# The gated transposition six products into the third part, and the lora products of the first two parts at eighteen products instead of twelve

## The reference

```python
# layer 0: one low-rank adapter (rank 16) per sequence
Bx  = einsum('bni,bri->bnr', x, B0[adapter_id])
x1  = x + einsum('bnr,bor->bno', Bx, A0[adapter_id])
# layer 1: a dense product and a gated mixture of 8 low-rank experts (rank 16)
base   = einsum('btd,od->bto', x1, W)
logits = einsum('btd,ed->bte', x1, Wr) + 5 * one_hot(lang_id)
gates  = softmax over the two largest logits, spread over the 8 experts
h      = einsum('btd,erd->bter', x1, A1)
out    = x1 + base + 2 * einsum('bter,bte,eor->bto', h, gates, B1)
```

## Time and profile before

| | |
|---|---|
| median of three runs | 525.92 us (523.71 to 525.93) |
| the profiled execution's own time | 527.19 us |
| its span, first to last instruction | 525.4 us |
| TensorE matmul busy | 510.3 us, 97% |
| VectorE busy | 382.2 us, 73% |
| ScalarE busy | 240.7 us, 46% |
| GpSimd busy | 172.2 us, 33% |
| mean granted TensorE clock | 0.997 of full speed |

### The profile page before, as it was taken

How to read it: one execution, slowest core, us unless ns; L and a number is a source line. 1 busy time by engine, 2 the same in 40 slices (tenths; PEclk the granted TensorE clock), 3 DMA queues, 4 the chain that set the end, 5 groups by cost and what they waited for, 6 DMA issues and landing times.

```text
span 525.4 us, 9426 instructions
## 1 busy us (share of the span) xinstructions
PE 510.3 (97%) x3350; PEld 464.4 (88%) x3350; DVE 382.2 (73%) x879; ACT 240.7 (46%) x543; POOL 172.2 (33%) x162
## 2 busy tenths in 40 slices
PE   6898999999999999999999999999999999999997
PEld 5787999878989899999989899998989999888997
DVE  3877786658669696977969697796969789694441
ACT  4645433445354544445454445455444545543221
POOL 6360325633414434132334414143442414330000
PEclk9999999999999999999999999999999999999999
DMA  8954255736667868567785857767675876632301
GB/s 331 311 132 110 90 133 170 205 112 217 227 186 204 243 179 253 177 210 238 249 246 150 252 182 232 233 210 248 180 234 177 249 207 211 201 120 82 121 40 41
DMA packets 52467, 99.76 MB, mean 190 GB/s; under 512 B 6716, under 2 KB 35260, under 8 KB 52420
## 3 DMA queue, kind: packets, MB, share of 16 engines
q1 hardware_dynamic: 45744, 78.14, 48.6%
q0 software_dynamic: 6656, 20.98, 12.3%
q10 hardware_dynamic: 20, 0.03, 0.0%
HBM read 69.24 MB, written 29.88 MB: 189 GB/s over the span
## 4 chain that ended last, share of the span: by engine, by line
PE 81%; DVE 10%; issue 4%; ACT 3%; another core or an unknown queue 1%; POOL 1%; DMA 0%; ACTq 0%; DVEq 0%
PE o_bank L601 64%; PE o_bank L614 8%; PE b_bank L493 2%; PE x_bank L521 2%; PE o_bank L590 2%; DVE a_raw L935 1%; PE b_bank L478 1%; ACT bx_pair L750 1%; DVE x_bank L900 1%; DVE b_raw L925 1%; PE o_bank L478 1%; PE x_bank L478 1%; DVE top_no L995 1%; ACT bx_swap L743 1%
## 5 line engine op out<-in xcount | busy, mean ns | idle before, releaser
L601 PE MATMUL o_bank<-w_hi,x_hi 128*128 128x512 f32 (+1 forms) x744 | 255.6, 344 | 0.0
L601 PE MATMUL o_bank<-w_lo,x_hi 128*128 128x512 f32 (+1 forms) x744 | 251.1, 337 | 0.0
L601 PE MATMUL o_bank<-w_hi,x_lo 128*128 128x512 f32 (+1 forms) x744 | 250.9, 337 | 0.0
L409 POOL TENSOR_TENSOR a_t<-a_raw,a_t 64x1024 fp32r<-64x1024 f32 x30 | 72.4, 2412 | 250.1 <-ACT a_t L723 177.5
L601 PEld LDWEIGHTS o_bank<-w_hi,x_hi 128*128 128x128 f32 x744 | 140.0, 188 | 13.4 <-issue 3.0
L601 PEld LDWEIGHTS o_bank<-w_lo,x_hi 128*128 128x128 f32 x744 | 139.9, 188 | 10.1
L601 PEld LDWEIGHTS o_bank<-w_hi,x_lo 128*128 128x128 f32 x744 | 139.7, 188 | 10.2
L380 POOL DMA_INDIRECT a_in<-in_L_cond_A_dram,a_run x64 | 60.9, 952 | 19.2 <-issue 18.7
L723 ACT CAST a_t<-a_raw 128x1024 fp32r<-128x1024 f32 x32 | 33.6, 1051 | 71.3 <-DVE a_raw L935 71.2
L935 DVE STREAM_TRANSPOSE a_raw<-a_in 128x1024 f32<-128x1024 f32 x32 | 65.3, 2045 | 0.0
L797 ACT COPY out_sb<-o_bank 128x376 f32<-128x376 f32 (+2 forms) x96 | 39.3, 443 | 54.4 <-PE o_bank L614 54.3
(11 more groups left out here) (110 smaller groups left out, 503.5 us busy)
## 6 DMA issues: line engine op xcount, KB each, us to landing
out_dram<-out_sb SPq DMA_DIRECT2D x31, 512.0 KB
x_in<-in_x_dram SPq DMA_DIRECT2D x120, 128.0 KB
w_in<-in_x_dram SPq DMA_DIRECT2D x25, 512.0 KB
x_dram<-w_in SPq DMA_DIRECT2D x25, 512.0 KB, 4.8
w_in<-x_dram SPq DMA_DIRECT2D x100, 128.0 KB
w_in<-in_L_cond_W_dram SPq DMA_DIRECT2D x6, 512.0 KB, 13.9
x_in<-in_x_dram SPq DMA_DIRECT2D x2, 512.0 KB
out_sb<-in_L_cond_W_dram SPq DMA_DIRECT2D x2, 512.0 KB, 14.6
```

What stands on the lines that cost most here:

```text
L409: nc.gpsimd.tensor_tensor(lower, a_raw[Q:P, m % 2, :], lower.bitcast(F32), ALU.subtract)\
L601: mm = pe.matmul(O[part][:, 0:hi - lo], xs[:, n % 2, c, :], w[:, c, lo:hi], start=(k == 0), stop=(k == K3 - 1), skip_group_check=True)
```

## The change

In every tile from 1 on, the first 6 products of part 2 are put ahead of `turn_gated`. The lora products of parts 0 and 1 stand 12 products behind the transposition, as they did, which is now at 18 of the 24 products of part 2, so that 6 of them are left behind instead of 12. Nothing is added or removed: TensorE has the same instructions in another order, and the orders of the other engines are as before. Tile 0, which is written out by itself, is not touched.

```diff
                 make_part(n, 1, 0, K3)
+                make_part(n, 2, 0, 6)
                 turn_gated(n)
-                make_part(n, 2, 0, 12)
+                make_part(n, 2, 6, 18)
                 pe.wait_ge(gt_ready, 2 * (n + 1))
                 add_lora(0)
                 add_lora(1)
-                make_part(n, 2, 12, K3)
+                make_part(n, 2, 18, K3)
                 add_lora(2)
```

## The result

The changed kernel takes 528.53 us (median of 15 runs, 526.50 to 531.18), the kernel before, beside it on the same chip, 525.69 (15 runs, 523.71 to 526.93): ratio 1.0059, 95% interval 1.0040 to 1.0078. It is slower by 2.8 us; forecast was 528.5. The profiled execution of after, 526.50 us with a span of 524.7, happens to be one of its two shortest, and is shorter than the profiled one of before. So the two traces must be compared stretch by stretch, not by their ends. That the forecast and the median agree to 0.03 us is luck in part: the interval of the ratio allows a change of 2.1 to 4.1 us.

A forecast was written before the change was run, and what follows sets the result against it. TensorE bounds the kernel (matmuls in 97% of the span). Early tiles −0.20, nine pairs +3.1, tile 28 −0.74 gave +2.1 us; without hold-ups +3.2; the middle, +2.6, gave 528.5 us, range 524.7 to 531.0.

The forecast's parts named there:

- The step, 0.89 us, and the delay of `gt_hi`: Six products put the transposition 0.89 us later; `gt_hi`, 0.31 behind it, moves 0.89 in odd tiles, 0.66 in even.
- A: Even tiles: TensorE's weight load for `make_x1` newly waits for GpSimd's late `a_t`; 0.15 us each, bounds 0 and 0.42.
- B: Even tiles: second half of the two-`make_bx` group newly waits for VectorE's `b_raw`; 0.19 us each, bounds 0 and 0.3.
- ScalarE's exponential behind the rounding of `a_t`: Even tiles: ScalarE's rounding, 0.89 us later, holds the exponential, which moves `gated` and L914 by 0.7.
- Later lora products cost nothing: Long regular stretch: next tile's `x_lo` and the copies out of PSUM come later but still in time, cost 0.
- The early tiles: Up to tile 9: tile 2 gains 0.47 us, tiles 4 and 5 nothing more, standing at −0.20 at tile 9.
- Tile 28: Two TensorE waits there are covered up to 0.89 us; `gt_lo` comes 0.15 later, so −0.74.
- The hold-ups look like chance: VectorE's in tiles 4 and 28, ScalarE's in 7: without them +3.2 us instead of +2.1; the middle, +2.6, taken.
- The signs: Trace: `gated` wait left in tile 5 alone, `gt_hi` waiting nearly everywhere, L493 group about 1.3, transposition distance +2.7 us.
- Rival 1: TensorE's waits for `gated` and `gt_lo` go and nothing replaces them: 3.9 us gained, 522.1 us; chance 0.07.
- rival 2: `a_t` and `b_raw` have room after all: only −0.3 to −1.2 us is left, about 525.2 us; chance 0.17.
- rival 3: Room is smaller, a pair costing 0.54, or hold-ups hit slackless paths: +4.0 to +5.3, about 530.5 us; chance 0.21.

The follow-up runs named there:

- fix6_odd: Changed kernel with VectorE's `gated_t_part` moved behind both halves L914 in odd tiles too, even tiles unaltered; 529.64 us, 1.0024 of the kernel before.
- odd6: Changed kernel with the move kept in odd tiles only, even tiles having transposition at 0 and lora at 12; 530.16 us, 1.0028 of the kernel before.
- even6: Changed kernel with transposition and lora products moved in even tiles only; 531.37 us, 1.0064 of the kernel before.
- turn0_lora18: Changed kernel with the transposition back ahead of part 2, only the lora products moved, to eighteen; 528.11 us, 0.9991 of the kernel before.
- early6: Changed kernel with the move kept in tiles 1 to 7 only; 529.83 us, 1.0012 of the kernel before.
- k3: Changed kernel with the transposition at 3 products into part 2 and lora at 15; 528.78 us, 0.9986 of the kernel before.
- fix0: VectorE's new order as in fix6, but with transposition at 0 and lora at 12 as before; 539.48 us, 1.0191 of the kernel before.
- fix6: Changed kernel with `gated_t_part` behind both halves L914 in odd tiles, in even ones also behind `x_lo`'s first half; 527.50 us, 0.9983 of before.
- turn6_lora12: Changed kernel with only the transposition moved, six products into part 2, lora staying at twelve; 533.27 us, 1.0093 of the kernel before.

## Why the prediction held, and where it did not

- *The step, 0.89 us, and the delay of `gt_hi`.* Right. `gt_hi` stands 0.31 behind the transposition in every tile from 6 on but 28 (2.03), with 0.99 of idle time before it in tile 17.
- *A, 0.15.* Right in place, cause and nearly in size. From the transposition of tile 17 to that of 18, where A lies and B does not, it is 319.52 − 304.81 = 14.71 us and was 320.24 − 305.64 = 14.60: 0.11. fix6_odd against after gives (245.58 − 244.87) / 8 = 0.09, odd6 0.10 with the longer L493 groups taken off. It is less than 0.15 because the product can follow its weight load by 0.03 (314.53 to 314.56), not only by the 0.18 of tile 8: it starts 0.27 behind the product ahead of it instead of 0.23, and the second product of L521 0.31 behind the first instead of 0.23, 0.12 together. The rival's upper end, 0.35 to 0.42, falls: the weight load starts 0.06 behind GpSimd's reported end, and 0.20 ahead of GpSimd's next start (314.73).
- *B, 0.19.* Right: the group grew by 0.19, from 1.08 to 1.27, which with the 0.11 makes up the 0.305 a pair, and even6 costs 0.20 a pair.
- *A and B do not overlap.* Right for the full change: 0.11 and 0.19 make up its 0.305 a pair, 2.44 us of 2.7 predicted. What I had not seen is that the odd transposition alone already costs 0.07 of B.
- *ScalarE's exponential behind the rounding of `a_t`.* Right: `half_sum` now waits for it in 11 places, 0.5 us each.
- *Later lora products cost nothing.* Right (turn0_lora18).
- *The early tiles, −0.20.* Neither shown nor refuted: early6's interval reaches from −0.5 to +1.7 us. In the traces the transposition of tile 10 is 142.13 us behind that of tile 1 in after, 143.40 in before, but before has the hold-ups of the earlier trace rows there and after has none.
- *Tile 28, −0.74.* Too large. With B of tile 26, 0.19, it should have made tiles 26 to 31 0.55 shorter; they are 0.26 shorter (75.42 to 75.16), and one wait of 0.57 for `gt_lo` stayed. I had `gt_lo` 0.15 later. What sets it there is VectorE held by GpSimd's `a_t` (last section), and that moves with A's chain.
- *The hold-ups look like chance, so take the middle.* +2.6 was the middle of +2.1 and +3.2; the medians differ by 2.84. They are not pure chance: see below. That the sum came out so close is luck: a pair costs a little less than forecast (0.305 for 0.34), tile 28 gave less than the 0.74, and the early tiles are open.
- *The signs.* The wait for `gated` fell to nothing and not to tile 5 alone, by 0.06 us. "DVE gt_hi <- PE L478" rose to 16 places, not to nearly every tile: from tile 8 on only odd tiles wait, 1.0 each and not 0.8, for in the even ones VectorE arrives just as the transposition ends. L521 shows its wait as "issue". The group of 1.27 (for 1.3) and the distance came as said.
- *Rival 1* falls by the waits that took the place of the ones removed; *rival 2* (the room is there) holds at three products (k3) and not at six; *rival 3* would have given a distance over 4 us longer.

## What to carry to other kernels

Moving a consumer later to give its producer time also delays everything that the producer's engine has queued behind the consumer's result. Before doing it, find on that engine the next results with a deadline, and measure the room of each: from the end of the result to the start of its user, and what the engine itself comes late behind the consumer. Here that is 0.78 − 0.06 = 0.7 us for `a_t`, and for `b_raw` 0.5 and the 0.23 by which VectorE came behind the transposition. The smallest room is how far the consumer may go, and nearly all that goes beyond is paid at every such place. Then move the producer's own order along: the same step cost 0.59% alone and gained 0.17% with VectorE's order fitted to it.

## What the runs showed of the hardware

**ScalarE, and perhaps VectorE, starts late where GpSimd has just begun to issue an indirect DMA.** The timeline of fix0, tile 9, all engines:

```profile
174.59 1.08 PE L493 MATMUL b_bank<-xt,b_raw 128*32 128x128 f32 x32
...
175.31 0.96 POOL L386 DMA_INDIRECT b_in<-in_L_cond_B_dram,b_run  x1 [0.75 <-POOL a_t L409]
...
176.57 0.95 POOL L380 DMA_INDIRECT a_in<-in_L_cond_A_dram,a_run  x1 [0.30 <-issue]
...
177.41 0.54 ACT L747 COPY bx_swap<-b_bank 64x128 f32<-64x128 f32 x2 [2.29 <-remote]
```

The same place of fix6:

```profile
173.86 1.08 PE L493 MATMUL b_bank<-xt,b_raw 128*32 128x128 f32 x32
...
174.57 2.39 POOL L409 TENSOR_TENSOR a_t<-a_raw,a_t 64x1024 fp32r<-64x1024 f32 x1 [6.79 <-DMA a_in<-in_L_cond_A_dram,a_run]
...
175.01 0.55 ACT L747 COPY bx_swap<-b_bank 64x128 f32<-64x128 f32 x2 [0.61 <-PE b_bank L493]
```

In fix6 the swap starts 0.07 us behind the end of the group (174.94), in fix0 1.74 behind it (175.67), and there GpSimd had begun to issue the gather of `b_in` 0.36 before that end. I counted this place over the 14 traces: ScalarE waited for `make_bx` 168 times. Where the group ended between 0.12 and 0.44 us behind the start of an issue, 16 times, the swap came 0.2 to 1.75 us late, 14 of them by over 1; in the other 152 it started within 0.08. Of these one group ended 0.03 behind the start of an issue and all others 7.7 or more, so the counts do not tell how far behind a start the hold reaches. VectorE's `gt_hi` shows something like it. Tile 4 of before, all engines; `gt_hi` itself starts at 105.42 there:

```profile
102.98 0.95 POOL L380 DMA_INDIRECT a_in<-in_L_cond_A_dram,a_run  x1 [0.30 <-issue]
103.11 1.28 DVE L875 TENSOR_TENSOR x_lo<-x_bank,x_hi 128x512 fp32r<-128x512 f32 x2
...
103.40 0.27 PE L478 MATMUL b_bank<-ident,gated 128*128 128x128 f32 x1
```

The transposition has ended at 103.67 and `x_lo` at 104.39, and still VectorE stands idle for 1.04. Where it waited idle for a transposition that ended less than 2 us behind the start of an issue, it stayed idle 0.85 to 1.5 us too long in 15 of 18 places (0.04 to 0.26 in the others); farther behind one, at most 0.05 in 152. But 13 of the 15 are this same place, tile 4, and after, the fourteenth trace, does not fit. There, too, the transposition of tile 4 ends 0.69 and `x_lo` 1.42 behind the start of the last issue, and `gt_hi` follows at once:

```profile
103.84 0.28 DVE L1022 CAST gt_hi<-b_bank 128x128 fp32r<-128x128 f32 x1
```

So an issue nearby is not enough for VectorE. For ScalarE's swap the late starts (the ones of 1.66 to 1.75 are called "remote", those of about 1.1 are put down to TensorE) go with GpSimd's issues without exception, and an order that shifts `make_bx` by a few tenths of a microsecond can meet them in tile after tile (fix0) or never (after). This is a coincidence over many traces; no kernel was run in which only the issue was moved. Whether the issue is the cause, and by what path, stays open.

**Two-input work on VectorE and GpSimd's `a_t` exclude each other.** Tile 6 of turn6_lora12, all engines, where `x_lo` of two halves takes 3.28 us instead of 1.28:

```profile
139.88 2.40 POOL L409 TENSOR_TENSOR a_t<-a_raw,a_t 64x1024 fp32r<-64x1024 f32 x1 [4.48 <-DMA a_in<-in_L_cond_A_dram,a_run]
...
140.17 3.28 DVE L879 TENSOR_TENSOR x_lo<-w_in,x_hi 128x512 fp32r<-128x512 f32 x2
...
146.04 0.65 PE L493 MATMUL b_bank<-xt,b_raw 128*32 128x128 f32 x16 [1.69 <-DVE b_raw L929]
```

The same tile of after, and its tile 28:

```profile
136.18 1.28 DVE L876 TENSOR_TENSOR x_lo<-w_in,x_hi 128x512 fp32r<-128x512 f32 x2
...
136.89 2.85 POOL L409 TENSOR_TENSOR a_t<-a_raw,a_t 64x1024 fp32r<-64x1024 f32 x1 [4.70 <-DMA a_in<-in_L_cond_A_dram,a_run]
...
469.50 2.40 POOL L409 TENSOR_TENSOR a_t<-a_raw,a_t 64x1024 fp32r<-64x1024 f32 x1 [1.60 <-ACT a_t L724]
...
469.99 1.93 DVE L1007 TENSOR_TENSOR weight<-weight,expd 128x1 f32<-128x1 f32 x1
```

Whoever starts first keeps its time and the other takes longer by about what is left: in turn6_lora12 `a_t` ends at 142.28, and 1.28 from there is 143.56, where `x_lo` ends at 143.45; in after `x_lo` ends at 137.46, and 2.41 from there is 139.87, where `a_t` ends at 139.74. In 7 of the 14 traces it was `x_lo` that lost, by 1.9 to 2.2 us. GpSimd's start there hangs on the landing of a gather (`a_in`), so a tenth of a microsecond decides who wins. The Trainium skill (SBUF — State Buffer, "SBUF: two separate sides") says just that: a VectorE operation in a 2-port mode or with two SBUF inputs and a GpSimd operation that reads SBUF take one port pair by an exclusive lock, for the whole instruction. The trace agrees for two inputs, with `x_lo` at 3.28 us instead of 1.28. In tile 28 every trace has it: in after a product of 128x1 that takes 0.16 elsewhere lasts until `a_t` is done (471.92 and 471.90); in before and seven others it is the CAST `top_no` ahead of it that is drawn out, to 1.7 to 2.2 us, so one SBUF input can be enough; whether that CAST runs in a 2-port mode no run here shows. That is what makes `gt_lo` late in tile 28. Moving GpSimd's `a_t` in tiles 6 and 28 was not tried.

Both effects turn small shifts into 1 to 2 us. They are a likely reason why executions of one kernel spread over 3 to 5 us, and why the profiled execution of after, the only one of the 14 without the hold-up of tile 4, could be shorter than that of before; that was not tested.
